# Where weights are loaded and who spreads a row to all partitions, in a graph layer with a mixture of experts

## The reference

```python
h = item_feat @ W_item.T + b_item
b = layernorm(x) @ W_user.T + b_user
x1 = x + relu(adj @ h + b)

xf = layernorm(x1)
probs = softmax(xf @ gate_w + gate_b)            # 8 experts
cw = probs where among the two largest, else 0
out = sum over experts e of cw[:, e] * (gelu(xf @ W1[e] + b1[e]) @ W2[e] + b2[e])   # 128 -> 256 -> 128
result = x1 + out
```

## Time and profile before

| | us |
|---|---|
| median of three runs | 1598.96 (1598.54 to 1600.05) |
| the profiled execution | 1599.19 |
| its span | 1597.1 |
| PE busy | 1572.8 (98%) |
| DVE busy | 1501.5 (94%) |
| ACT busy | 1233.5 (77%) |
| loads of raw | 780 of 500 KB, 5.2 us from issue to landing |
| spreads | 160 of the scales, 80 of the moments, 250 KB each, 4.9 to 6.7 us |
| DMA, all | 488.31 MB, mean 306 GB/s |

### The profile page before, as it was taken

How to read it: one execution, slowest core, us unless ns; L and a number is a source line. 1 busy time by engine, 2 the same in 40 slices (tenths; PEclk the granted TensorE clock), 3 DMA queues, 4 the chain that set the end, 5 groups by cost and what they waited for, 6 DMA issues and landing times.

```text
span 1597.1 us, 26128 instructions
## 1 busy us (share of the span) xinstructions
PE 1572.8 (98%) x7105; PEld 1307.2 (82%) x7105; DVE 1501.5 (94%) x2169; ACT 1233.5 (77%) x1440; POOL 68.6 (4%) x63
## 2 busy tenths in 40 slices
PE   7989999999999999999999999999999999999997
PEld 6868888888888888888888888888888888888875
DVE  6989999999999999999999999999999999999987
ACT  5768787777878787778787878777787787877866
POOL 2000000000000000000000000000000000000000
PEclk9999999999999999999999999999999999999999
DMA  9989998999998989898989898989999999989962
GB/s 368 362 307 312 313 312 308 320 303 318 311 321 296 330 286 332 292 332 284 339 279 352 276 344 282 342 291 327 294 325 311 311 312 309 318 304 314 309 208 78
DMA packets 168373, 488.31 MB, mean 306 GB/s; under 512 B 26097, under 2 KB 63858, under 8 KB 168354
## 3 DMA queue, kind: packets, MB, share of 16 engines
q1 hardware_dynamic: 156576, 479.61, 87.6%
q10 hardware_dynamic: 10946, 6.17, 1.2%
q0 software_dynamic: 832, 2.30, 0.4%
HBM read 481.90 MB, written 6.10 MB: 306 GB/s over the span
## 4 chain that ended last, share of the span: by engine, by line
issue 93%; PE 2%; DMA 2%; POOL 1%; DVE 1%; SPq 0%; ACT 0%; POOLq 0%; DVEq 0%; ACTq 0%
POOL moments_sb L442 1%; DMA raw<-in_adj_main 1%; PE acc L918 0%; PE acc L919 0%; PE acc L920 0%; DVE t_sb L781 0%; DVE o_sb L792 0%; DMA r_sb<-t_moments_rows 0%; DMA spread_sb<-scales 0%; ACT a_hi L480 0%; DVE a_lo L773 0%; DVE a_lo L654 0%; DMA t_moments_rows<-turned_sb 0%; SPq L345 0%; PE ps_y L889 0%
## 5 line engine op out<-in xcount | busy, mean ns | idle before, releaser
L480 ACT ACTIVATE a_hi<-raw 128x1000 fp32r<-128x1000 f32 (+1 forms) x800 | 805.1, 1026 | 266.0 <-PE acc L920 188.6
L654 DVE TENSOR_TENSOR a_lo<-raw,a_hi 128x1000 fp32r<-128x1000 f32 x780 | 917.8, 1192 | 43.7 <-ACT a_hi L480 42.0
L918 PE MATMUL acc<-a_hi,h_hi 128*128 128x500 f32 x1560 | 610.3, 391 | 7.7 <-DVE a_lo L654 6.9
L920 PE MATMUL acc<-a_hi,h_lo 128*128 128x500 f32 x1560 | 608.3, 390 | 0.0
L919 PE MATMUL acc<-a_lo,h_hi 128*128 128x500 f32 x1560 | 606.3, 389 | 0.0
L918 PEld LDWEIGHTS acc<-a_hi,h_hi 128*128 128x128 f32 x1560 | 293.8, 188 | 68.2 <-DVE a_lo L654 5.4
L920 PEld LDWEIGHTS acc<-a_hi,h_lo 128*128 128x128 f32 x1560 | 293.9, 188 | 60.7
L919 PEld LDWEIGHTS acc<-a_lo,h_hi 128*128 128x128 f32 x1560 | 294.3, 189 | 59.3
L531 ACT ACTIVATE g_sb<-ps_z,b_sb 128x500 f32<-128x500 f32 x304 | 188.2, 670 | 64.2 <-PE ps_y L941 62.1
L773 DVE TENSOR_TENSOR g_lo<-g_sb,g_hi 128x1000 fp32r<-128x1000 f32 x152 | 180.9, 1190 | 4.0 <-ACT g_hi L537 3.9
L537 ACT ACTIVATE g_hi<-g_sb 128x1000 fp32r<-128x1000 f32 x152 | 156.3, 1029 | 0.1
(11 more groups left out here) (142 smaller groups left out, 909.2 us busy)
## 6 DMA issues: line engine op xcount, KB each, us to landing
raw<-in_adj_main SPq DMA_DIRECT2D x780, 500.0 KB, 5.2
spread_sb<-scales SPq DMA_DIRECT2D x160, 250.0 KB, 6.0
xr_sb<-in_xR SPq DMA_DIRECT2D x20, 256.0 KB, 7.3
x_sb<-in_xT SPq DMA_DIRECT2D x20, 250.0 KB, 7.2
xr_sb<-u_moments_rows SPq DMA_DIRECT2D x20, 250.0 KB, 5.3
r_sb<-u_moments_rows SPq DMA_DIRECT2D x20, 250.0 KB, 6.7
xt_sb<-t_moments_rows SPq DMA_DIRECT2D x20, 250.0 KB, 4.9
r_sb<-t_moments_rows SPq DMA_DIRECT2D x20, 250.0 KB, 5.8
```

The costliest lines, as they stand in the source:

```text
L480: nc.scalar.activation(a_hi[q][0:rows, 0:cols], raw[s][0:rows, 0:cols], ACT.Copy).then_inc(hi_ready, 1)
L654: nc.vector.tensor_tensor(low, whole, val(high), ALU.subtract).then_inc(lo_ready, 1)
L918: nc.tensor.matmul(acc[:, 0:T], w_hi, m_hi, start=(k == 0), stop=False)
L920: last = nc.tensor.matmul(acc[:, 0:T], w_lo, m_hi, start=False, stop=False)
```

## The change

Four things are changed.

1. POOL issues the constants and W1 only when PE has used three positions (WEIGHTS_FROM = 3).
2. The spreads of moments and scales are issued by ACT, at positions 8 (S_TAIL), 20 (S_USER) and 31, 41, 42, 43, 46 (S_SPREAD). SP only loads. Spreads of the last tail, tail(20), and the scales behind the loop stay with SP.
3. The last tail's scales have rows of their own in DRAM (`last_scales`), and their store doesn't wait for the scaling of expert (19, 7).
4. The orders behind the loop are changed on ACT, DVE and PE. In `up(i, 0)` the product with xn_lo comes last, behind a wait of its own, so that the other four of its six products need xn_hi alone.

```diff
-S_SPREAD = (36, 36, 36, 36, 43, 44, 46, 50)
+S_SPREAD = (31, 31, 31, 31, 41, 42, 43, 46)
+WEIGHTS_FROM = 3
-S_TAIL, S_USER = 13, 25
+S_TAIL, S_USER = 8, 20
...
+        last_scales = nc.dram_tensor("last_scales", (E * Q, TQ), fp32).ap()
...
+            pool.wait_ge(adj_used, WEIGHTS_FROM)
             for dst, src in consts:
                 pool.dma_start(dst[:, :], src).then_inc(const_landed, 16)
...
-                    since(act, scaled, expert(i, 0))
-                    act.dma_start(scales.rearrange("r (b j) -> b r j", j=SQ), cwT_sb[:, :]).then_inc(cw_stored, 16)
+                    if not is_last(i):
+                        since(act, scaled, expert(i, 0))
+                    act.dma_start(scales_at(i).rearrange("r (b j) -> b r j", j=SQ), cwT_sb[:, :]).then_inc(cw_stored, 16)
+
+            def spread_tail(i, p):
+
+                if p == S_TAIL:
+                    act.wait_ge(t_stored, i * 16)
+                    act.dma_start(xt_sb[:, 0:T], columns(t_moments_rows, 0)).then_inc(t_spread, 16)
+                    act.dma_start(r_sb[:, :], columns(t_moments_rows, 2)).then_inc(t_spread, 16)
...
+            def spread(i, p):
+                for e in range(E):
+                    if p != S_SPREAD[e]:
+                        continue
+                    if e == 0:
+                        act.wait_ge(cw_stored, i * 16)
+                    since(act, scaled, expert(i, e) - (SPREADS - 1))
+                    act.dma_start(spread_sb[e % SPREADS][:, :],
+                                 scales_of(i, e)).then_inc(spread_landed[e % SPREADS], 16)
...
                     if with_tail:
                         tail(i, p)
+                        spread_tail(i, p)
                     if with_finish:
                         experts(i - 1, p + NPOS)
+                        spread(i - 1, p + NPOS)
                         if p == A_STORE:
                             finish(i)
                     if with_tail:
                         experts(i, p)
+                        spread(i, p)
                     user(i, p)
+                    spread_moments(i, p)
...
-            tail(NB, A_NORM)
-            high(rest, 7)
+            high(rest, 7)
+            tail(NB, A_NORM)
             tail(NB, A_EXP)
             gelu(NB, 0)
             high(NB, 0)
+            tail(NB, A_SEND)
             gelu(NB, 1)
-            tail(NB, A_SEND)
             high(NB, 1)
...
             tail(NB, V_STATS)
+            tail(NB, V_NORM)
             scale(rest, 3)
-            tail(NB, V_NORM)
+            low(rest, 5)
             scale(rest, 4)
             add(rest, 3)
-            low(rest, 5)
+            add(rest, 4)
+            scale(rest, 5)
             low(rest, 6)
-            add(rest, 4)
             tail(NB, V_XN)
-            scale(rest, 5)
+            low(rest, 7)
             tail(NB, V_LOGITS)
-            add(rest, 5)
             tail(NB, V_LO)
-            low(rest, 7)
-            scale(rest, 6)
             tail(NB, V_PROB)
-            add(rest, 6)
             tail(NB, V_COMPARE)
             tail(NB, V_RANK)
             tail(NB, V_WEIGHT)
+            scale(rest, 6)
             low(NB, 0)
+            add(rest, 5)
             scale(rest, 7)
+            add(rest, 6)
             add(rest, 7)
...
                     pe.wait_ge(xn_hi_ready, i)
-                    pe.wait_ge(xn_lo_ready, i)
...
+                if e == 0:
+
+                    pe.wait_ge(xn_lo_ready, i)
+                    for j in range(HH):
+                        up_low(e, j)
...
             rest = NB - 1
+            down(rest, 3)
             tail(NB, T_TURN)
-            down(rest, 3)
```

More of the change, by code:

```diff
@@ L206, in build @@
         u_moments_rows = nc.dram_tensor("u_moments_rows", (SQ, TQ), fp32).ap()
-        scales_of = scales.rearrange("(e q) t -> e (q t)", q=Q)
+        last_scales = nc.dram_tensor("last_scales", (E * Q, TQ), fp32).ap()
         gt_sb = xt_sb[0:TQ, 0:Q * E * E]
@@ L313, in is_last, with scales_at, scales_of @@
             return isinstance(i, int) and i == NB
+        def scales_at(i):
+            return last_scales if is_last(i) else scales
+        def scales_of(i, e):
+            return scales_at(i).rearrange("(e q) t -> e (q t)", q=Q)[e, 0:T].partition_broadcast(P)
         def y_banks(i):
@@ L361, in load_x @@
                 sp.dma_start(x_sb[:, :], xT[i]).then_inc(x_landed, 16)
[L363 to L376, removed]
             for p in range(NPOS):
@@ L386, in _, with one_pass @@
                     load_x(0)
-                spread_moments(0, p)
+            def one_pass(i):
+                for p in range(NPOS):
+                    load_step(i, p)
+                    if p == S_ROWS:
+                        sp.wait_ge(u_dense, i)
+                        load_xr(i)
+                    if p == RAW:
+                        sp.wait_ge(x1_ready, i)
+                        load_x(i)
+            def spread_tail(i, p):
+                if p == S_TAIL:
+                    sp.wait_ge(t_stored, i * 16)
+                    sp.dma_start(xt_sb[:, 0:T], columns(t_moments_rows, 0)).then_inc(t_spread, 16)
+                    sp.dma_start(r_sb[:, :], columns(t_moments_rows, 2)).then_inc(t_spread, 16)
             def spread(i, p):
@@ L396, in spread @@
                     sp.dma_start(spread_sb[e % SPREADS][:, :],
[L397 to L418, removed]
+                                 scales_of(i, e)).then_inc(spread_landed[e % SPREADS], 16)
+            with sp.Fori(1, NB) as i:
+                one_pass(i)
             for p in range(NPOS):
@@ L521, in tail, with spread_tail, spread_moments @@
                     act.wait_ge(cwT_ready, i)
-                    since(act, scaled, expert(i, 0))
-                    act.dma_start(scales.rearrange("r (b j) -> b r j", j=SQ), cwT_sb[:, :]).then_inc(cw_stored, 16)
+                    if not is_last(i):
+                        since(act, scaled, expert(i, 0))
+                    act.dma_start(scales_at(i).rearrange("r (b j) -> b r j", j=SQ), cwT_sb[:, :]).then_inc(cw_stored, 16)
+            def spread_tail(i, p):
+                if p == S_TAIL:
+                    act.wait_ge(t_stored, i * 16)
+                    act.dma_start(xt_sb[:, 0:T], columns(t_moments_rows, 0)).then_inc(t_spread, 16)
+                    act.dma_start(r_sb[:, :], columns(t_moments_rows, 2)).then_inc(t_spread, 16)
+            def spread_moments(i, p):
+                if p == S_USER:
+                    act.wait_ge(u_stored, i * 16 + 16)
+                    since(act, xn_ready, i)
+                    act.dma_start(xr_sb[:, 0:T], columns(u_moments_rows, 0)).then_inc(u_spread, 16)
+                    act.dma_start(r_sb[:, :], columns(u_moments_rows, 2)).then_inc(u_spread, 16)
+            def spread(i, p):
[6 more added lines that the diff above has]
+                    act.dma_start(spread_sb[e % SPREADS][:, :],
+                                 scales_of(i, e)).then_inc(spread_landed[e % SPREADS], 16)
             def gelu(i, e):
@@ L587, in _ @@
             high(NB, 0)
+            tail(NB, A_SEND)
             gelu(NB, 1)
-            tail(NB, A_SEND)
             high(NB, 1)
             gelu(NB, 2)
+            high(NB, 2)
             finish(NB)
-            high(NB, 2)
             gelu(NB, 3)
@@ L853, in _ @@
             scale(NB, 1)
+            low(NB, 3)
             add(NB, 0)
-            low(NB, 3)
+            add(NB, 1)
             scale(NB, 2)
-            add(NB, 1)
             low(NB, 4)
@@ L863, in _ @@
             scale(NB, 4)
+            low(NB, 6)
             add(NB, 4)
-            low(NB, 6)
             scale(NB, 5)
@@ L967, in up, with up_low @@
                     nc.tensor.matmul(ps_z[j][:, 0:T], w1_hi[:, at:at + P], xn_hi[:, :], start=True, stop=False)
-                    nc.tensor.matmul(ps_z[j][:, 0:T], w1_hi[:, at:at + P], xn_lo[:, :], start=False, stop=False)
-                    nc.tensor.matmul(ps_z[j][:, 0:T], w1_lo[:, at:at + P], xn_hi[:, :], start=False,
-                                     stop=True).then_inc(z_done, 1)
+                    nc.tensor.matmul(ps_z[j][:, 0:T], w1_lo[:, at:at + P], xn_hi[:, :], start=False, stop=False)
+                    if e > 0:
+                        up_low(e, j)
+                if e == 0:
+                    pe.wait_ge(xn_lo_ready, i)
+                    for j in range(HH):
+                        up_low(e, j)
+            def up_low(e, j):
+                at = e * H + j * P
+                nc.tensor.matmul(ps_z[j][:, 0:T], w1_hi[:, at:at + P], xn_lo[:, :], start=False,
+                                 stop=True).then_inc(z_done, 1)
             def experts(i, p):
```

## The result

The changed kernel takes 1602.09 us (median of 22 runs) against 1598.48 us of the kernel before (22 runs): 1.0024 times as long, 95% interval 1.0018 to 1.0030. It is slower by some 3.6 us. The forecast was 1594.3 us with a range to 1600.0, so the sign was wrong. The profiled execution took 1603.95 us around a span of 1602.1 us, 5.0 us more than the span before.

The account below looks back on a forecast made before the run. TensorE was taken as busy throughout middle blocks, so gains lay only at the start, block 1 and the end. 1599.19 - 0.25 (start) - 3.5 (block 1) - 0 (middle) - 1.1 (end) = 1594.34, stated as 1594.3 us; range 1592.0 to 1600.0.

Parts of the forecast that it names:

- Middle blocks: Blocks after block 1: moving twelve DMA issues from SP to ACT costs 0 us; bound 9.5 us lost over 19 blocks.
- the burst: ACT's four spread issues in a row at position 31: taken as 2.29 us as on SP, causing no TensorE wait.
- rival A: Middle blocks: ACT's burst or the spreads' traffic delays position 34's tile; 1603.8 us, or 1598.1 at 0.2 us each; chance 0.15.
- the slack of 0.58: Middle blocks: TensorE uses position 34's result 0.58 us after it is ready; 0.3 us used, 0.3 left.
- Block 1: ACT issuing the moments' spreads wins 3.5 us in block 1, including 1.7 us of clock; bounds 0.4 and 4.6.
- what stands in the way of the two spreads: Block 1: on ACT's queue spreads share engines with loads instead of lying behind them, taking 4.5 to 5 us, not 6.5.
- The 1.7 us of clock: Block 1: neither TensorE wait is near 3 us, so no half clock is expected, winning 1.7 us.
- Rival B: Block 1: ACT only takes SP's place in line, spreads take 6.5 us again, 0 to 0.4 won; 1597.6 us; chance 0.26.
- Start: Block 0: late weights bring position 3 2.4 us sooner, but only 0.25 us reaches the block's end.
- The bytes are only postponed, so position 27 lands when it did: Block 0: queue stays backed up until 70 us, so only 0.25 of the 2.4 us won remains.
- rival C: Block 0: the start's gain is kept because position 27's loads come sooner, 2 us more; 1592.3 us; chance 0.11.
- End: Behind block 19: new orders and own rows for the last scales win 1.1 us; bounds 0 and 1.6.

Follow-up runs that it names:

- e3: Kernel before with only the spreads of moments and scales issued by ACT, at the changed kernel's positions: 1604.0 us, ratio 1.0041.
- e4: Changed kernel with the eight spreads of the scales issued by SP again, moments still on ACT: 1598.16 us, ratio 1.0001.
- e5: Changed kernel with ACT's first four scale spreads at positions 31, 32, 35 and 37 instead of all at 31: 1597.83 us, ratio 0.9999.
- e8: Changed kernel with scales on SP, moments on ACT, and SP waiting in block 1 for the moments' store ahead of load 14: 1597.95 us, ratio 1.0000.
- e11: Changed kernel with scales on SP, moments on ACT, and SP held ahead of load 14 in block 1 until both spreads landed: 1594.9 us, ratio 0.9981.
- e6: Changed kernel with all spreads issued by SP at the positions of before, leaving late weights and the new end: 1595.65 us, ratio 0.9980.
- e10: Changed kernel with ACT's burst split over 31, 32, 35, 37 and the tail's two spreads on SP at position 13: 1595.33 us, ratio 0.9985.
- e1: Kernel before with only the late loads of constants and W1: 1596.56 us, ratio 0.9989.
- e9: Changed kernel, all spreads on SP, block 1's tail spreads issued behind load 11 or 12 instead of 13: 1594.61 us (11), 1592.98 us (12).
- e2: Kernel before with only the new order behind the loop, own rows for the last scales and late xn_lo product: 1597.2 us, ratio 0.9994.
- e7: Changed kernel with ACT's four spreads at position 31 cut to 8 of 500 columns, SP issuing the rest at 36: 1600.0 us, ratio 1.0013.

## Why the prediction was wrong

**Middle blocks: the step that failed.** I costed the burst at nothing because SP's row of four measured 2.29 us, and called it decided at 2.6 us. The mechanism of rival A was right in each link (position 32 late, then DVE's tile of position 34, then TensorE) and its chance of 0.15 far too low. Two sizes were off. First, the threshold is about 2.3 us and not 2.6. My sum put position 32 at 298.0 and position 33 at 300.1, 2.3 and 4.4 us behind position 31, and so left 0.3 us of the slack of 0.58. It left out most of what passes besides the issues: 0.08 us before the first of them and 0.18 behind the last. In block 2, with a burst of 2.31 us, position 32 begins 2.57 and position 33 4.64 us behind position 31, against 4.07 before: 0.57 of the 0.58 us are gone. The row of 2.29 that I took for safe lay at the threshold. Second, ACT's bursts average 2.51 us in this profile (2.33 in e3's) against SP's 2.13. With a spread of issue times from 0.32 to 0.74 us in the earlier trace rows a sum of four needed a margin that was not there. Forecast 0; measured +6.1 us in the profile and 3.9 to 4.3 us in the medians (e4, e5).

**Block 1: wrong.** The hold of ACT, the wait of 0.9 us at position 9 (0.79) and the unchanged store (5.7 us) came as worked out. The step that failed is "what stands in the way of the two spreads": I let them gain from leaving SP's queue. The loads issued before them were in front either way (in e8 loads 11 to 13 still land every 1.2 us, at 101.1, 102.3 and 103.6, and the first spread at 105.0), and the loads issued behind them became rivals. 4.5 to 5 us were forecast, 7.6 measured, and the wait before position 12 stayed at 2.99 us, with twice as much half clock behind it (a mean of 0.76 over 106 to 120 us against 0.88; in four of the six profiles with the pair on ACT it was 0.88 too). The 1.7 us of clock that I had counted as won did not come. Of the Trainium skill (DMA: Bandwidth & Descriptors, Queues, rings and completion order) I had taken that the engines take turns between queues. e8 and e11 agree with it for the loads behind the spreads, 3.7 us on r_sb; for those in front no gain showed. Rival B had the right idea but a lower bound of nothing lost; the move cost 2.2 us (e5 against e6; 2.5 by e10 for the tail's pair alone).

**Start: right in sign, too small.** Position 3 came at 18.16 us where 18.1 was forecast, but in part by luck: the wait of 1.47 us before position 1, most of which was to go, stayed, and position 0 began 0.39 us sooner (10.69 for 11.08 us), which was not in the sum. "The bytes are only postponed, so position 27 lands when it did" failed. With late weights and the spreads on SP the tile landed at 60.2 to 61.3 us (e1, e6, e9), with early weights at 61.3 to 62.8 (before, e2, e3). The likely cause is that the engines moved more in the first 17 us (349 GB/s in e1 against 314); no run tests it by itself. 0.25 forecast, 1.5 to 1.8 us measured, inside the bound of 2.4. It was rival C, at 0.11.

**End: right.** 1.1 us forecast; 0.9 to 1.0 us in e2, though not clear of noise there, 1.4 us over the profiles, 1.7 us in the changed kernel's. xn came at 11.96 us behind the relu (12.5 forecast), low(20,0) at 20.0 (20.9), and DVE's gap for the scales went with the own rows.

With the measured terms the sum reads 1595.65 (e6, start and end) + 2.2 (moments, e5 against e6) + 4.3 (the burst, the changed kernel against e5) = 1602.1 us. These are differences of medians and add up by construction; what tests them is that e6 came out as e1 and e2 together say, and that e3 has the whole loss.

## What to carry to other kernels

Moving DMA issues to an engine that computes costs it their time in its own line, and a row of them can cost more than any single one. Take the slack of the tightest position and the longest row, not the median, and spread the issues over positions. A small transfer that someone waits for should be ahead of the bulk loads on the same queue; on a queue of its own it shares the engines with every load sent after it. One profile of a place where the clock can fall says little about a few microseconds: look at the granted clock behind the wait before comparing two. Bytes postponed out of a stretch where the engines are badly used are not just moved, they can be won.

## What the runs showed of the hardware that I had not expected

ACT's issues in a row got longer. Of four whole spreads in a row they averaged 0.35, 0.42, 0.69 and 0.86 us (longest 1.69), and with a sixtieth of the bytes still 0.35, 0.42, 0.67 and 0.56 (e7). SP's four in the kernel before averaged 0.45, 0.37, 0.53 and 0.45. The single one at position 31 of e5 took 0.33 to 0.35 us.

Two spreads of 250 KB landed 5.2 and 8.2 us after their issue with one stream of loads going on behind them, and 3.8 and 4.5 us after it without (e8 and e11).

Behind nearly equal waits of 3.24 and 3.12 us TensorE kept its full clock once (e10) and lost it once (e5), and that made 2.7 us of block 1.
